# Attention's out product in a hybrid transformer layer: one product of 512 columns for both parts of W_o, and its two halves added to the rows one by one

## What is computed

```python
x = x + attn_a(_layernorm(x), gamma, w_qkva)          # rms norm, projections, gated scan: stage A
x = x + ffn(_layernorm(x), W1, b1, W2, b2)            # ternary weights, exact gelu: stage B
x = x + attn_b(_layernorm(x), W_q, W_k, W_v, W_o)     # stage C
x = x + ffn(_layernorm(x), W1, b1, W2, b2)            # stage D
```

```python
k_C = k_t @ C_QV
G = G + outer(k_t, k_C)
S_K = S_K + outer(k_t, k_t)
C_QV = C_QV + outer(q_t, v_t)
o_t = q_t @ (S_K @ C_QV - G)
```

## Time and profile before

| | |
|---|---|
| median of three runs | 1054.02 us |
| lowest, highest | 1047.87, 1054.55 us |
| profiled execution | 1044.3 us |
| its span, first to last instruction | 1042.3 us |
| PE busy | 1008.8 us, 97% |
| DVE busy | 616.8 us, 59% |
| ACT busy | 491.5 us, 47% |
| POOL busy | 111.7 us, 11% |
| mean granted clock of TensorE | 0.994 of full speed |

### The profile page before, as it was taken

The page is one execution under the profiler, slowest core; times in us unless marked ns, Lnnn a source line. Parts: engine busy times, 40 slices in busy tenths (PEclk is TensorE's granted clock), DMA queues, the critical chain, the costliest instruction groups (busy, mean ns, idle before and its releaser), DMA issues.

```text
span 1042.3 us, 42204 instructions
## 1 busy us (share of the span) xinstructions
PE 1008.8 (97%) x19166; PEld 909.8 (87%) x19166; DVE 616.8 (59%) x1252; ACT 491.5 (47%) x925; POOL 111.7 (11%) x130
## 2 busy tenths in 40 slices
PE   8997999998999999999999999999999999999998
PEld 6786689898889999999999899889998998789897
DVE  7787677771444554464555554554554546757773
ACT  5675666652433443343334334343443344556663
POOL 2460313310000000000000000000000000113130
PEclk9999999999999999999999999999999999999999
DMA  9420100011343343234333423432343243300101
GB/s 313 159 50 1 81 1 1 0 64 60 122 125 96 92 129 100 84 120 121 92 104 108 120 84 103 123 106 84 104 124 104 90 137 105 84 21 21 42 31 51
DMA packets 60733, 92.71 MB, mean 89 GB/s; under 512 B 7056, under 2 KB 50448, under 8 KB 59536
## 3 DMA queue, kind: packets, MB, share of 16 engines
q1 hardware_dynamic: 60288, 90.07, 27.8%
q10 hardware_dynamic: 272, 0.00, 0.0%
HBM read 48.63 MB, written 41.42 MB: 86 GB/s over the span
## 4 chain that ended last, share of the span: by engine, by line
PE 74%; issue 1%; DVE 1%; ACT 1%; POOL 0%; POOLq 0%
PE bank L215 7%; PE bank L216 6%; PE bank L217 6%; PE bank L1163 6%; PE bank L1189 6%; PE bank L1174 5%; PE bank L1223 3%; PE bank L1211 3%; PE bank L1153 3%; PE bank L1200 3%; PE bank L1225 3%; PE bank L1239 3%; PE bank L1224 3%; PE bank L1155 3%; PE bank L1154 3%; PE bank L1257 3%
## 5 line engine op out<-in xcount | busy, mean ns | idle before, releaser
L1581 DVE STREAM_TRANSPOSE k<-kt 128x512 f32<-128x512 f32 x64 | 43.4, 696 | 110.2 <-ACT kt L1440 58.6
L1445 ACT COPY qt<-bank 128x512 f32<-128x512 f32 x64 | 37.5, 586 | 148.1 <-PE bank L217 148.1
L1440 ACT COPY kt<-bank 128x512 f32<-128x512 f32 x64 | 37.5, 586 | 116.7 <-PE bank L217 116.7
L1602 DVE TENSOR_TENSOR state_s<-bank,state_s 128x256 f32<-128x256 f32 x124 | 46.7, 419 | 70.5 <-ACT ut L1458 68.5
L215 PE MATMUL bank<-ln_xhi,wk_hi 128*128 128x256 f32 x256 | 76.1, 297 | 3.4 <-POOL state_z L1097 3.4
L1223 PE MATMUL bank<-wo_hi,ot_hi 128*128 128x256 f32 x256 | 75.0, 293 | 1.0 <-issue 1.0
L215 PE MATMUL bank<-ln_xhi,wq_hi 128*128 128x256 f32 x256 | 75.4, 295 | 0.0
L217 PE MATMUL bank<-ln_xhi,wk_lo 128*128 128x256 f32 x256 | 72.5, 283 | 1.7 <-issue 1.7
L1492 ACT ACTIVATE D_hidden<-bank,b_sb 128x512 f32<-128x512 f32 x64 | 44.1, 689 | 60.8 <-PE bank L1240 60.8
L216 PE MATMUL bank<-ln_xlo,wk_hi 128*128 128x256 f32 x256 | 72.6, 283 | 0.0
L216 PE MATMUL bank<-ln_xlo,wq_hi 128*128 128x256 f32 x256 | 72.5, 283 | 0.0
(11 more groups left out here) (161 smaller groups left out, 2926.5 us busy)
## 6 DMA issues: line engine op xcount, KB each, us to landing
k_rows_scratch<-k SPq DMA_DIRECT2D x32, 512.0 KB, 2.9
k<-k_rows_scratch SPq DMA_DIRECT2D x128, 128.0 KB, 3.6
u_rows_scratch<-sc_and_k SPq DMA_DIRECT2D x31, 512.0 KB, 3.1
landed<-u_rows_scratch SPq DMA_DIRECT2D x124, 128.0 KB, 3.4
out_dram<-xres SPq DMA_DIRECT2D x16, 256.0 KB, 2.1
xres<-in_L_attn_a_x_dram SPq DMA_DIRECT2D x7, 512.0 KB, 10.0
w_nat<-in_L_ffn_W_dram SPq DMA_DIRECT2D x2, 1024.0 KB, 9.6
raw<-in_L_attn_b_W_q_dram SPq DMA_DIRECT2D x1, 1024.0 KB, 12.5
```

## The change

W_o's two parts are kept side by side for each pair of heads, in one tile `wo_both` [128, 8, 2, 256]. In the out product, o's high part meets both in one product of 512 columns: o_hi·W_hi goes to columns 0 to 255 of the bank and o_hi·W_lo to columns 256 to 511. o_lo·W_hi is a product of 256 columns as before, onto columns 0 to 255. DVE adds first the one half of the columns to the rows, for batch rows 0 and 1, and then the other half; each of the later adds waits for the earlier one on the same rows (`half_added`). `x_added` now counts two for an out product, and all that wait for it wait for twice the number.

```diff
-        wo_hi = sbuf(outer, "wo_hi", [P, PAIRS * D], FP32R)
-        wo_lo = sbuf(outer, "wo_lo", [P, PAIRS * D], FP32R)
+        wo_both = sbuf(outer, "wo_both", [P, PAIRS, 2, D], FP32R)
+        wo_hi, wo_lo = wo_both[:, :, 0, :], wo_both[:, :, 1, :]
...
+                if SPLITS[m] == "o":
+                    return [(src[:, n * BLK:(n + 1) * BLK].rearrange("p (n d) -> p n d", d=D),
+                             wo_hi[:, 2 * n:2 * n + 2, :], wo_lo[:, 2 * n:2 * n + 2, :]) for n in range(4)]
+                hi, lo = wv_hi[:, :, :].rearrange(flat), wv_lo[:, :, :].rearrange(flat)
...
-            out_ready, x_added = sem("C_out"), sem("C_xadd")
+            out_ready, half_added, x_added = sem("C_out"), sem("C_halfadd"), sem("C_xadd")
...
                 def out_product(i):
 
-                    dst = bank[out_bank(i)][:, 0:D]
+                    dst = bank[out_bank(i)]
                     pe.wait_ge(o_low, 2 * (i + 1))
                     for p in range(PAIRS):
-                        w = [x[:, p * D:(p + 1) * D] for x in (wo_hi, wo_lo)]
-                        nc.tensor.matmul(dst, ot_hi[:, p, :], w[0], start=(p == 0), stop=False)
-                        nc.tensor.matmul(dst, ot_hi[:, p, :], w[1], start=False, stop=False)
-                        last = nc.tensor.matmul(dst, ot_lo[:, p, :], w[0], start=False, stop=(p == PAIRS - 1))
+                        nc.tensor.matmul(dst[:, :], ot_hi[:, p, :], wo_both[:, p, :, :].rearrange("p w d -> p (w d)"),
+                                         start=(p == 0), stop=False, skip_group_check=True)
+                        last = nc.tensor.matmul(dst[:, 0:D], ot_lo[:, p, :], wo_hi[:, p, :], start=False,
+                                                stop=(p == PAIRS - 1), skip_group_check=True)
                     last.then_inc(out_ready, 1)
...
                     elif j:
-                        pe.wait_ge(x_added, j - 1)
+                        pe.wait_ge(x_added, 2 * (j - 1))
...
                     if norm_of(j) or j == CHUNKS - 1:
-                        pe.wait_ge(x_added, j - 1)
+                        pe.wait_ge(x_added, 2 * (j - 1))
...
                 def add_out(i):
                     dve.wait_ge(out_ready, i + 1)
-                    for b in range(B):
-                        at = (b * TILES + i // 2) * D
-                        row = xres[half(i % 2), at:at + D]
-                        last = nc.vector.tensor_tensor(row, bank[out_bank(i)][half(b), 0:D], row, ALU.add)
-                    last.then_inc(x_added, 1)
+                    for w in range(2):
+                        for b in range(B):
+                            if w:
+                                dve.wait_ge(half_added, 2 * i + b + 1)
+                            at = (b * TILES + i // 2) * D
+                            row = xres[half(i % 2), at:at + D]
+                            nc.vector.tensor_tensor(row, bank[out_bank(i)][half(b), w * D:(w + 1) * D], row, ALU.add)\
+                                .then_inc(x_added if w else half_added, 1)
```

More of the change, by code:

```diff
@@ L287, in split_pieces @@
                              ring(wk_hi, n), ring(wk_lo, n)) for n in range(4)]
-                hi, lo = (wv_hi[:, :, :].rearrange(flat), wv_lo[:, :, :].rearrange(flat)) if SPLITS[m] == "v" else (wo_hi, wo_lo)
+                if SPLITS[m] == "o":
+                    return [(src[:, n * BLK:(n + 1) * BLK].rearrange("p (n d) -> p n d", d=D),
+                             wo_hi[:, 2 * n:2 * n + 2, :], wo_lo[:, 2 * n:2 * n + 2, :]) for n in range(4)]
+                hi, lo = wv_hi[:, :, :].rearrange(flat), wv_lo[:, :, :].rearrange(flat)
                 cut = [slice(n * BLK, (n + 1) * BLK) for n in range(4)]
@@ L1297, in first_group @@
                             if j > 3:
-                                pe.wait_ge(x_added, j - 2)
+                                pe.wait_ge(x_added, 2 * (j - 2))
                             if norm_of(j - 1) and norm_of(j - 1) < 2 * NBLK:
@@ L1426, in _ @@
                             if t == 1:
-                                pe.wait_ge(x_added, CHUNKS)
+                                pe.wait_ge(x_added, 2 * (CHUNKS))
                             prepare(target[0], nd + target[1])
@@ L1695, in _ @@
                         if norm_of(j + 1) == 2 * NBLK:
-                            dve.wait_ge(x_added, 8)
+                            dve.wait_ge(x_added, 2 * (8))
                             ln.dve_statistics(dve, 0, 0, nd)
```

## The result

The changed kernel takes 1068.0 us in the median of four runs, the kernel before 1052.8: a ratio of 1.0145, with an interval of 1.0102 to 1.0187, or 15.2 us more. Timed again beside later experiments it was 1066.4 against 1048.6, a ratio of 1.0153 (1.0113 to 1.0193). The forecast was 1070, slower by 16.6 us. A ratio here is not the quotient of the two medians; the two differ by up to 0.2%.

A forecast was written before the change was run, and what follows sets the result against it. PE, busy 97%, was taken to bound the kernel, so its waits for the adds lengthen the span: 13.8 + 3.4 - 0.6 = +16.6 us on the median 1054.0 gives 1070, range 1059 to 1077.

The forecast's parts named there:

- Even chunks: PE's wait for the adds between by_states' batch rows, 16 chunks: each 0.86 us longer, 13.8 us lost (10.9 to 15.4).
- the 0.05 from add to PE: At the wait between by_states' batch rows, PE goes on 0.05 us after the last add ends.
- nothing in reserve: In even chunks PE already waits for the adds between batch rows, a 0.13 us step, so any delay reaches PE.
- These waits cost nothing: On DVE, adds 3 and 4 wait for 1 and 2, whose increments come early enough: 0 us.
- Norm chunks: Seven odd chunks whose transposes wait for the adds: 0.37 of 0.86 us absorbed, 0.49 each, 3.4 us lost (2.2 to 4.1).
- Other odd chunks, chunk 31, W_o's layout: DVE idle time covers later adds, chunk 31 by a tenth; splitting W_o on POOL is unchanged: cost 0.
- The products: Out products on PE: joining 256-column pairs into 512 wins 0.6 us over 32 (4.4 won to 1.2 lost).
- Rival C: Loads pace PE, so wide products run at a narrow one's pace: 13 us faster, 1041; chance 0.03.
- Sum: Whole kernel: stalls of 13.8 and 3.4 less 0.6 won, +16.6 us (8.7 to 20.7).
- No clock effect is in play: Whole profile before: the clock row is at its upper level, 2.4 GHz, in all 40 slices.
- Rival A: A waiting PE lets instruction supply catch up, issue stops (6.0 us) vanish: +10.6 us, 1065; chance 0.13.
- Rival B: DVE later: adds paced by own waits, 0.96 a chunk, masks 0.2 late in 15 odd chunks; about 1077; chance 0.13.

The follow-up runs named there:

- the first experiment: Against the changed kernel: wide product kept, only columns 0 to 255 added, with the two adds of before; 1051.7 us against 1049.5 for the kernel before, ratio 1.0036.

## Why the prediction was right

The time was right within 2 us, the sign and the mechanism as forecast, and the terms of the sum nearly so. Three small errors partly cancel: two costs came out larger, by 0.9 and 0.8 us, and so did the gain, by 0.8.

- *Even chunks.* Forecast 16 x 0.86 = 13.8. Measured: the step grew by 0.92, 16 x 0.92 = 14.7. The place, the 0.05 from add to PE and "nothing in reserve" held. Mis-sized by 0.06: three steps between four adds are 0.45 and not 0.43, since now every add signals. "These waits cost nothing" was nearly right for the waits (the step from the second to the third add, the first that waits, is 0.458, the others 0.448) and wrong for the increments.
- *Norm chunks.* Forecast 7 x 0.49 = 3.4. Measured: the transposes start 0.56 later behind the adds' start, and since the adds start by DVE's own order there, the 0.04 that the out product ends earlier comes on top for PE: 7 x 0.60 = 4.2. The step in front of the transposes' first load grew from 0.20 to 0.81 in all seven.
- *Other odd chunks, chunk 31, W_o's layout.* Forecast 0. No wait for the adds or for the masks of sc_b is new in them; the one such wait, 1.6 us once, was there before.
- *The products.* Forecast 0.6 won. Measured: 2.770 instead of 2.813 per out product, 32 x 0.043 = 1.4 won. Rival C is out: the wide product steps at 0.229.
- *Sum.* 14.7 + 4.2 - 1.4 = 17.5, forecast 16.6; the medians give 15.2 and 17.8.

The two profiled executions differ by more, 1066.4 - 1042.3 = 24.1 us. The rest is for the most part the stops at issue, 14.0 against 8.0, and one stretch of 3.4 us at the lower clock. "No clock effect is in play" holds for stage C of that one profile, not for the kernel: a digit of 9 stands for 90% or more, and three stretches of 13.8 us together, at 102, 242 and 1041 us, are at the lower level. Rival A, that a PE which waits lets the supply catch up, did not come: in no profile with the new waits are these stops fewer than in that of before. That they are more is shown only against the one fast profile of before; the first experiment, without the new waits, has as many. Rival B's extra 0.2 in all odd chunks did not come either. Its other half, a dearer add, did in part: 0.92 of its 0.96.

## What to carry to other kernels

A wait that costs 0.1 us is in no list of waits and may still be the one that binds: look at the steps between instruction starts on both sides of it, and compare a place where the wait is absent. Before a result is spread over more columns or more instructions, ask who gets the bank next and when; where it has nothing in reserve, that engine pays for each instruction of the evacuation, while joining two products into one of the same columns saved only 5 ns here. A wait belongs in front of the first write that needs it, not in front of the group.

## What the runs showed that I had not expected

PE's stops at issue keep to blocks of 256 instructions in all profiles, and some come back at the same block for the same program: in both profiles of the changed kernel at 12152 with 1.9 and 2.2 us, at 35448 with 2.6 each. The page has a queue of its own for instructions, in the kernel before:

```profile
q8 instruction: 149, 2.44, 1.0%
```

149 packets of 16.4 KB. The stop at 35448 in the changed kernel falls into a stretch in which the other transfers are dense (columns: PE, PEld, DVE, ACT, POOL busy; granted clock; DMA share; GB/s):

```profile
908.00:912.00 4.00, 1.61 (x114) 1.48 (x104) 1.95 (x4) 0.00 (x0) 0.00 (x0) 1.00 0.64 126
912.00:916.00 4.00, 4.00 (x25) 2.83 (x28) 1.54 (x3) 1.37 (x3) 0.00 (x0) 0.57 0.02 4
```

That a late packet behind these transfers is the cause was not tested. The second row shows what such a stop can drag along: PE stood still for 2.4 us, and then the granted clock was at its lower level (1.2 GHz) for most of the next 4. The products of 512 columns there step at 0.43 instead of 0.23:

```profile
913.29 0.63 PE L1242 MATMUL bank<-ln_xhi,D_w1t 128*128 128x512 f32 x1
913.71 0.63 PE L1243 MATMUL bank<-ln_xlo,D_w1t 128*128 128x512 f32 x1
914.14 0.63 PE L1242 MATMUL bank<-ln_xhi,D_w1t 128*128 128x512 f32 x1
```

No stretch between 246 and 1041 us of the kernel before was at that level in its profile. The new waits for the adds, under 1.1 us each, did not bring the clock down in either profile of the changed kernel: its four such stretches in stage C lie at stops at issue.
